# Mask products of the scores on half of the array's rows, two units' masks issued together

## The reference: what is computed

```python
q = apply_rope(heads(x @ Wq.T)); k = apply_rope(heads(x @ Wk.T)); v = heads(x @ Wv.T)   # 16 heads of 16
scores = einsum('bhqd,bhkd->bhqk', q, k) / sqrt(16)
scores = where(tril(ones(256, 256)), scores, -inf)     # the causal mask
out = einsum('bhqk,bhkd->bhqd', softmax(scores), v) @ Wo.T
```

## Time and profile before

| | us |
|---|---|
| median of three runs | 624.12 (622.48 to 624.27) |
| profiled execution, device time | 621.83 |
| its span in the trace | 619.9 |
| PE busy in the span | 572.3 (92%) |
| DVE busy | 462.2 (75%) |
| ACT busy | 336.1 (54%) |
| POOL busy | 231.7 (37%) |

### The profile page before, as it was taken

One profiled execution on the slowest core, in us unless ns is written; L12 is line 12 of the kernel. 1 busy time (PEld: TensorE's weight loads), 2 busy tenths in 40 slices (PEclk: granted clock), 3 DMA queues, 4 the chain that ended last, 5 costly groups with the idle time before them and its releaser, 6 DMA issues. The chain is left out here.

```text
span 619.9 us, 17941 instructions
## 1 busy us (share of the span) xinstructions
PE 572.3 (92%) x6596; PEld 500.3 (81%) x6596; DVE 462.2 (75%) x943; ACT 336.1 (54%) x595; POOL 231.7 (37%) x446
## 2 busy tenths in 40 slices
PE   1899999998679999999999999999987899999997
PEld 1788888888668888888888888887765788888886
DVE  5977777787488888888878797877643677777764
ACT  2665444444227667766667666567554554444442
POOL 6383333332546453543545445433120333333310
PEclk9999999998889999999999999999999899999999
DMA  8430000000777666555665556657300011111111
GB/s 266 141 103 2 0 0 0 0 0 1 186 206 197 191 173 189 161 152 173 179 195 163 158 149 173 187 159 202 107 4 1 1 34 34 34 34 34 34 34 35
DMA packets 71141, 63.43 MB, mean 102 GB/s; under 512 B 4130, under 2 KB 64322, under 8 KB 71106
## 3 DMA queue, kind: packets, MB, share of 16 engines
q1 hardware_dynamic: 69769, 62.74, 34.9%
q10 hardware_dynamic: 1337, 0.21, 0.3%
HBM read 33.03 MB, written 29.36 MB: 101 GB/s over the span
## 5 line engine op out<-in xcount | busy, mean ns | idle before, releaser
L782 DVE TENSOR_REDUCE mx<-bank 128x2 f32<-128x512 f32 (+1 forms) x192 | 118.5, 682 | 33.2 <-PE bank L967 33.2
L498 PE MATMUL bank<-w2q,g_hi 128*128 128x256 f32 x512 | 123.9, 284 | 1.5 <-DVE g_lo L326 1.1
L420 ACT ACTIVATE g<-bank,b1c 128x512 f32<-128x512 f32 x128 | 88.3, 691 | 64.6 <-PE bank L492 61.6
L498 PE MATMUL bank<-w2q,g_lo 128*128 128x256 f32 x512 | 122.0, 280 | 0.0
L894 ACT ACTIVATE probs<-bank 128x512 f32<-128x512 f32 x192 | 111.1, 597 | 9.5 <-PE bank L967 1.6
L498 PEld LDWEIGHTS bank<-w2q,g_hi 128*128 128x128 f32 x512 | 96.5, 189 | 3.1 <-DVE w2q L336 1.2
L498 PEld LDWEIGHTS bank<-w2q,g_lo 128*128 128x128 f32 x512 | 96.5, 188 | 0.7
L265 POOL TENSOR_TENSOR res<-res,b2h 128x1024 f32 (+1 forms) x16 | 38.4, 2400 | 145.1 <-DVE xn L146 119.7
L326 DVE TENSOR_TENSOR g_lo<-g,g_hi 128x512 fp32r<-128x512 f32 x128 | 83.8, 686 | 3.4
L492 PE MATMUL bank<-xt_hi,w1q 128*128 128x512 f32 x240 | 76.7, 401 | 3.3 <-DVE xt_lo L166 1.8
L492 PE MATMUL bank<-xt_lo,w1q 128*128 128x512 f32 x240 | 76.1, 398 | 0.0
(11 more groups left out here) (129 smaller groups left out, 1149.9 us busy)
## 6 DMA issues: line engine op xcount, KB each, us to landing
qk_slots<-parts SPq DMA_DIRECT2D x32, 384.0 KB, 3.6
q<-qk_slots SPq DMA_DIRECT2D x32, 384.0 KB, 3.8
k<-qk_slots SPq DMA_DIRECT2D x32, 384.0 KB, 4.8
qk_slots<-parts SPq DMA_DIRECT2D x32, 256.0 KB, 3.0
res<-x SPq DMA_DIRECT2D x8, 512.0 KB, 3.6
qk_slots<-parts SPq DMA_DIRECT2D x32, 128.0 KB, 3.2
out<-res SPq DMA_DIRECT2D x8, 512.0 KB, 2.9
w1f<-w1t SPq DMA_DIRECT2D x2, 512.0 KB, 6.6
```

Of the source, the lines that this page charges most:

```text
L420: nc.scalar.activation(g[:, f, :], h_bank[f % 4][:], ACT.Gelu, bias=b1c[:, f:f + 1]).then_inc(g_ready, 1)
L498: last = nc.tensor.matmul(to[:, 0:D], part[:, f, t * P:(t + 1) * P], w2q[:, f, :], start=f == 0 and part is g_hi, stop=f == FC - 1 and par ...
L782: nc.vector.tensor_reduce(o, i, AX.X, ALU.max).then_inc(s_done, 1)
```

## The change

1. `fence` gets an argument `rows` and uses 64 rows of the array instead of 128: a 64 x 64 block of the identity as weights, and the diagonal block of the mask that lies on the same 64 partitions. S takes rows 0 to 63, T takes rows 64 to 127.
2. S and T are each cut into a wait, a mask and the products. Step n is now: both waits, both masks (four instructions, on the four 64 x 64 quarters of the array), the products of S(n), the products of T(n). The waits are followed by an increment of a new semaphore, `rings_free`, that nobody waits for.
3. In T the unit of four heads comes first in its group (`T_PIECE = (2, 0, 1)`), so that the masks issued together have the same width: 256 columns and 256, or 128 and 128. ACT follows with the pieces in the same order.

```diff
+T_PIECE = (2, 0, 1)
+    rings_free = sem("att_rings_free")
             def exponentials(p, h):
-                    g, u = n // 3, n % 3
+                    g, u = n // 3, T_PIECE[n % 3]
-            def fence(to, mask):
+            def fence(to, mask, rows):
+                r = bass.ts(rows, HALF_ARRAY)
                 for c in range(HALVES):
                     c = bass.ts(c, HALF_ARRAY)
-                    nc.tensor.matmul(to[c, :, c], ident_b[:, c], mask[:, :, c], start=True, stop=False, skip_group_check=True)
+                    nc.tensor.matmul(to[c, :, c], ident_b[r, r], mask[r, :, r], start=True, stop=False, skip_group_check=True)
...
+            def fence_S(n):
+                u = n % 3
+                if u == 0:
+                    fence(s_ring[u][:].rearrange("p (a k) -> p a k", a=4), mask_qk[:, 0:4, :], 0)
+                else:
+                    fence(s_ring[u][:].rearrange("p (a k) -> p a k", a=2)[:, :, P:SEQ], mask_qk[:, 0:2, :], 0)
...
+            def fence_T(n):
+                u = T_PIECE[n % 3]
+                r = t_ring[n % 2]
+                if u < 2:
+                    fence(r[:].rearrange("p (a q) -> p a q", a=2)[:, :, 0:P], mask_kq[:, 0:2, :], 1)
+                else:
+                    fence(r[:].rearrange("p (a q) -> p a q", a=4), mask_kq[:, 0:4, :], 1)
...
             def step(p, h):
                 for n in range(6 * h, 6 * h + 6):
+                    if p.has(1):
+                        wait_S(p, n)
+                    if p.has(0):
+                        wait_T(p, n)
+                    if p.has(1) or p.has(0):
+                        pe.sem_inc(rings_free, 1)
+                    if p.has(1):
+                        fence_S(n)
+                    if p.has(0):
+                        fence_T(n)
                     if p.has(1):
                         S(p, n)
                     if p.has(0):
```

More of the change, by code:

```diff
@@ L968, in halves, with wait_S @@
                 return last
-            def S(p, n):
-                b, par, g, u = p.p + 1, p.parity(1), n // 3, n % 3
+            def wait_S(p, n):
+                b, par = p.p + 1, p.parity(1)
                 if n == 0 and not p.has(-1):
@@ L979, in S @@
                     pe.wait_ge(mt_sb, 2 * b + n // 6)
-                r, q, k = s_ring[n % 3], q6[par], k6[par]
+            def fence_S(n):
+                u = n % 3
                 if u == 0:
-                    fence(r[:].rearrange("p (a k) -> p a k", a=4), mask_qk[:, 0:4, :])
+                    fence(s_ring[u][:].rearrange("p (a k) -> p a k", a=4), mask_qk[:, 0:4, :], 0)
+                else:
+                    fence(s_ring[u][:].rearrange("p (a k) -> p a k", a=2)[:, :, P:SEQ], mask_qk[:, 0:2, :], 0)
+            def S(p, n):
+                par, g, u = p.parity(1), n // 3, n % 3
+                r, q, k = s_ring[u], q6[par], k6[par]
+                if u == 0:
                     for j in range(4):
@@ L986, in S @@
                 else:
-                    fence(r[:].rearrange("p (a k) -> p a k", a=2)[:, :, P:SEQ], mask_qk[:, 0:2, :])
                     for j in range(2):
@@ L991, in S, with wait_T @@
                 last.then_inc(s_ready, 1)
-            def T(p, n):
-                b, par, g, u = p.p, p.par, n // 3, n % 3
+            def wait_T(p, n):
+                b, par = p.p, p.par
                 if n % 6 == 0:
@@ L998, in T @@
                     pe.wait_ge(t_done, UNITS * b + n - 1)
+            def fence_T(n):
[5 more added lines that the diff above has]
+                    fence(r[:].rearrange("p (a q) -> p a q", a=4), mask_kq[:, 0:4, :], 1)
+            def T(p, n):
+                par, g, u = p.par, n // 3, T_PIECE[n % 3]
                 r, q, k = t_ring[n % 2], q6[par], k6[par]
                 if u < 2:
-                    fence(r[:].rearrange("p (a q) -> p a q", a=2)[:, :, 0:P], mask_kq[:, 0:2, :])
                     for j in range(2):
@@ L1005, in T @@
                 else:
-                    fence(r[:].rearrange("p (a q) -> p a q", a=4), mask_kq[:, 0:4, :])
                     for j in range(4):
```

## The result

The changed kernel takes 657.61 us in the median of four runs (656.22 to 661.67), the kernel before 623.83 (622.48 to 624.27): a ratio of 1.0556, 95% interval 1.0506 to 1.0607, or +33.8 us. The profiled execution of the changed kernel took 661.67 us, the highest of its four, that of the kernel before 621.83; so the two traces lie 39.8 us apart, 6 more than the medians.

The account below looks back on a forecast made before the run. PE was taken to bound the attention, with ACT setting the pace inside bursts. Full bursts 28.3, DVE's lateness 1.5 and bursts of T alone 0.6 gave +30.4 us: 652.2 profiled, median 654.5, range 635 to 676.

Parts of the forecast that it names:

- The term of the full bursts: The 30 bursts with both S and T: +0.96 us each, less 0.5 for the first, 28.3 us.
- The first burst: Held 1.05 us by a copy of maxima; 0.5 of its growth was taken to go into that hold.
- The 1.5 us for DVE's lateness behind the bursts: DVE's last maxima end 0.1 later than PE's shift, costing at most 0.1 in 15 halves.
- The bursts of S alone: The two bursts paced by DVE at 0.61 per unit against PE's 0.54: no growth.
- Change of shape, 0.105 from three changes of columns: Switching PE between mask and product tiles costs 0.105 us each time, bounds 0 and 0.21.
- Four masks in 0.11: A step's four side-by-side masks take 0.11 us even when narrow, 0.13 after a wait or change of shape.
- The floor of the prediction: Lowest time for a narrow step's masks on PE: 0.06 us, making the sum 8 us smaller.
- Who sets the pace: Within a burst, PE's own step of 0.79 sets the pace, just above the 0.77 chain through ACT.
- The increment at nothing: One more instruction on PE's queue per step: at least 0, at most 0.10 us, taken as 0.
- Rival A: Changes of rows nearly free, only the earlier wait costs: +0.34 to +0.37 a burst; 634 to 642 us, chance 0.18.
- Rival B: Changes of shape or increment cost more: increment 0.10 a step, or weight loads +1.2 a burst; 662 to 690, chance 0.22.
- Rival C: Faster, 610 us: masks shrink 0.46 a burst, if shape changes cost under 0.04 and chain under two times 0.59; chance 0.06.

Follow-up runs that it names:

- e8 to e11: Kernel before with T(0) ahead of S(0), 623.78 us; also T's four-head unit first, 624.10; layer norm statistics last alone, 622.21; T(0) first and statistics last, 621.18.
- e1: Changed kernel with its masks put back on all 128 rows, waits first and increment kept: 646.82 us, ratio 1.0393.
- e2: Changed kernel with masks on all 128 rows and without the increment of rings_free: 643.13 us, ratio 1.0334.
- e7: Changed kernel with each exponential cut to 128 of 512 columns: 651.52 us, against 621.87 for the kernel before with the same cut.
- e5: Changed kernel with T's units in their old order (0, 1, 2): 664.36 us, ratio 1.0659 to the kernel before.
- e4: Kernel before, in its order, with masks on 64 rows and an increment ahead of each mask: 705.51 us, ratio 1.1349.

## Why the prediction was right, step by step

**The size.** Forecast +30.4, measured +33.8. The term of the full bursts was 28.3; the trace shows 30.1, +1.0 a burst as worked out (0.96). The first burst, which is held by a copy of maxima, grew by 0.66 (from 5.09 to 5.75), where 0.46 was allowed; but it takes 4.43 to 5.36 in e8 to e11, which don't have the change, so its growth says little. The 1.5 us for DVE's lateness behind the bursts did not come: the stretches stayed at 6.18 and 5.02. DVE's maxima end 5.37 after the burst's start (266.16) instead of 4.36, which is 1.01 later, as much as PE itself is late; the prediction had DVE later by 1.06 and PE by 0.96. The bursts of S alone were put at nothing and those of T alone at 0.6; they grew by 1.6 and 2.3, mostly in the stretches at the 1.2 GHz level, which the sum did not have. At full clock the one burst of T alone grew by 0.5.

**Change of shape, 0.105 from three changes of columns: right.** 0.11 to 0.12 in the kernel with rows alone. The first step of a burst gives it as foretold: the first T's products start 0.48 after the burst's start (260.79 to 261.27), where 0.35 would have meant no cost. The drain that the Trainium skill names (TensorEngine Tiling (Array Packing), Key Properties) is what every such gap here agrees with. But the gap is also as long as a weight load (0.11), and no run tells the two apart: in the kernel before the weight load of a mask can start 0.10 ahead of its product, in the changed kernel, at a change of shape, it starts with it (261.59 in both engines' timelines).

```profile
252.65 0.11 PEld L962 LDWEIGHTS bank<-mask_qk,ident_b 128*64 128x64 bf16 x2
252.75 0.22 PE L962 MATMUL bank<-mask_qk,ident_b 128*64 128x128 bf16 x2
```

```profile
261.59 0.11 PEld L965 LDWEIGHTS bank<-mask_qk,ident_b 64*64 64x64 bf16 x2
```

**Four masks in 0.11: wrong for the narrow steps.** They start together and take the time of the columns: 0.18 from mask to products, less 0.11 for the change, is 0.07. The floor of the prediction was the right value, and the rate of the products beside them was not a limit. That tiles start almost together is what the Trainium skill states (TensorE: Matmul & The Clock Gate, Measured speedup vs the span model), and the trace agrees: 0.00 to 0.01 between the two kinds of masks. PE's stream in a burst is 4.56, not 4.74.

**Who sets the pace: wrong.** The prediction had PE at 0.79 per step and the chain through ACT at 0.77. It is the reverse. In the changed kernel masks start 0.14 after an exponential's end, three times in the burst shown; only with the exponentials cut does PE's stream set the pace. The chain is the term that was mis-sized, by the next point: 0.60 + 0.14 + 0.18 + 0.24 + 0.22 + 0.21 = 1.59 for two narrow steps against 1.54.

**The increment at nothing: wrong.** With it the wait stands on an instruction of its own, and the mask starts 0.14 instead of 0.05 after a met wait. That is 0.09 each time; e1 and e2 are 3.7 us apart, without any change of shape. It was argued that the gap of the change would cover it; but mask starts are 0.14 behind the exponential both in e1, which has no change of shape, and in the changed kernel, so it is the change of shape that the wait covers, and the 0.09 comes after the wait. Nor would leaving out the increment alone have saved it everywhere: in e2 two waits ahead of one mask cost the same 0.09 in 20 of 30 bursts.

These errors had opposite signs: the stream was put at 4.74 a burst and is 4.56, and the chain, which was to add nothing, adds 0.23. So the burst came out near the 4.74 forecast, at 4.79 (4.82 in the mean of the 29 behind the first), and that the size fits so well is partly luck. The sign rested on something firmer: both ways of costing it, stream and chain, led to a longer burst, and e7 and e1 show each of them to do it alone. Rival A (free changes of shape) had its mechanism right and under-priced it: +0.36 per burst with masks side by side; e2, with the same waits and the masks one after the other, has 0.55 to 0.8. Rival B had the right size for the increment (0.10 a step) but charged it in every step; it shows only where a wait is met. Rival C fell on its first condition, 0.04 per change of shape, and on its second.

**Left open.** Why the granted clock fell in the ends of the attention in the profiled execution of the changed kernel so much more than in that of the kernel before (0.50 and 0.50 against 0.81 and 1.00). In e1 it stayed at 1.00 in both places; in e5, the changed kernel in another order, it fell in both again (0.61 from 171 to 183 us, 0.55 from 500 to 512); in e7 it fell only in the first (0.50 from 171 to 182, 1.00 from 490 to 502) and in e4, with twice the changes of shape, in neither. The spread of the changed kernel's runs (656.22 to 661.67) fits a loss that comes and goes, but no run isolates it. Whether the changed kernel needs the increment stays open too: no run has a product on 64 x 64 that waits on a register itself.

## What to carry to other kernels

A mask on half of the array's rows is worth what it saves only if it leaves the array's shape alone: here two changes of shape per step, 0.22 us, stood against a saving of 0.05 us in a narrow step (two masks of 0.06 against 0.07 for both) and 0.10 in a wide one (two of 0.11 against 0.12). Before moving a wait forward in an in-order stream, write down the chain that goes through its buffer (here exponential, mask, products, exponential, two steps of 0.61) and add to it what the wait now stands in front of; if the engine at its other end has no slack in that stretch, the product moved behind the wait is paid in full. Count, too, what each wait rides on: two waits ahead of one product can put one of them on an instruction of its own, which here delayed every product behind a met wait by 0.09 us. And read the slack in the stretch, not in the average: ACT was busy 54% of the span and had no gap in the burst.

## What the runs showed of the hardware

- A change between 64 x 64 and 128 x 64 tiles costs 0.11 to 0.12 us in each direction (e4), as much as a change of columns (128 x 32 to 128 x 64, 128 x 64 to 128 x 128: 0.10 to 0.11 in the earlier trace rows).
- Four products on the four quarters of the array, two banks, with their weight loads, take about the time of one pair on all rows: 0.07 us for 128 columns (0.18 from mask to products less 0.11 for the change of shape) where the pair takes 0.06 in the earlier trace rows. They start within 0.01 us of each other.
- On PE, a mask whose weight load carries the wait itself starts 0.05 us after the end of the exponential that it waits for. With the wait on a semaphore instruction of its own it starts after 0.14 us, with an increment on that instruction (e1, the changed kernel) or without (20 of 30 bursts of e2). Where the wait is long met nothing shows: from T's products to the next mask, with that instruction between, the changed kernel's unwaited steps take 0.32, as much as from T's products to the transposes behind a burst in the earlier trace rows, with no increment between.
